# Attention scratch and SiLU results moved from PSUM to SBUF in a two-layer token kernel

## What is computed

```python
kx = modulated_linear(x, s, k_aff_w, k_aff_b, k_w, k_b).reshape(B, N, H, D)
scores = einsum('bnhd,bnjd->bnhj', kx, kx) / sqrt(D)       # 16 x 16 for each token
A = softmax(scores, axis=-1)
out = einsum('bnhj,bnjd->bnhd', A, kx).reshape(B, N, F)
x = x + modulated_linear(out, s, o_aff_w, o_aff_b, o_w, o_b)
...
x = x + _ln(silu(cat @ int_W1 + int_b1) @ int_W2 + int_b2) # cat: the six parts
```

## Time and profile before

| | us |
|---|---|
| median of three runs | 875.09 |
| lowest and highest of the three | 874.53, 875.51 |
| the profiled execution, measured from outside | 875.09 |
| its span, from the first to the last instruction | 873.2 |

### The profile page before, as it was taken

One profiled execution on the slowest core, in us unless ns is written; L12 is line 12 of the kernel. 1 busy time (PEld: TensorE's weight loads), 2 busy tenths in 40 slices (PEclk: granted clock), 3 DMA queues, 4 the chain that ended last, 5 costly groups with the idle time before them and its releaser, 6 DMA issues.

```text
span 873.2 us, 19685 instructions
## 1 busy us (share of the span) xinstructions
PE 843.7 (97%) x7456; PEld 768.8 (88%) x7474; DVE 644.7 (74%) x1067; ACT 488.3 (56%) x851; POOL 608.1 (70%) x766
## 2 busy tenths in 40 slices
PE   5996999999999999999999999999999999999997
PEld 5854888989999998989999898999999898999986
DVE  3589777778787867679797877679797767677652
ACT  3567555565656465465656556465647546464531
POOL 2377999678786766768776866768777775756472
PEclk9898999999999999999999999999999999999999
DMA  8972234425343333425243332424333342323110
GB/s 285 418 255 61 71 86 119 115 57 153 77 153 84 98 92 85 127 50 158 69 149 89 108 92 73 115 71 146 83 122 91 86 116 49 104 67 82 47 50 25
DMA packets 104365, 95.55 MB, mean 109 GB/s; under 512 B 72880, under 2 KB 78160, under 8 KB 102608
## 3 DMA queue, kind: packets, MB, share of 16 engines
q1 hardware_dynamic: 95056, 69.26, 27.6%
q0 software_dynamic: 4608, 16.78, 7.0%
q10 hardware_dynamic: 4608, 8.25, 2.8%
HBM read 69.60 MB, written 8.40 MB: 89 GB/s over the span
## 4 chain that ended last, share of the span: by engine, by line
PE 91%; DVE 4%; DMA 2%; issue 1%; ACT 1%; ACTq 0%; SPq 0%; POOL 0%; another core or an unknown queue 0%; DVEq 0%; POOLq 0%
PE acc L399 45%; PE tok L399 29%; PE att L399 8%; PE xp L552 6%; PE xp L399 3%; DMA kb<-in_kb 1%; DVE stg_e L1277 1%; DMA BD<-q 0%; DVE raw_k L1164 0%; SPq L297 0%; DVE W1xl L1267 0%; DVE q L1290 0%; DVE BD L1179 0%; DVE qt L1283 0%
## 5 line engine op out<-in xcount | busy, mean ns | idle before, releaser
L1699 POOL TENSOR_TENSOR op1l<-ytmp,op1h 128x512 fp32r<-128x512 f32 x64 | 90.3, 1411 | 20.8 <-ACT op1h L906 20.4
L1645 POOL TENSOR_TENSOR xlo<-xraw,xhi 128x512 fp32r<-128x512 f32 x31 | 40.8, 1317 | 68.6 <-ACT xhi L798 68.6
L399 PE MATMUL acc<-op0h,W1xh 128*128 128x256 f32 x256 | 75.8, 296 | 1.4 <-DVE op0l L1369 1.1
L399 PE MATMUL acc<-op1h,W1th 128*128 128x256 f32 x256 | 75.0, 293 | 0.0
L399 PE MATMUL acc<-op1h,W1hh 128*128 128x256 f32 x256 | 73.7, 288 | 0.0
L399 PE MATMUL acc<-op0h,W1sh 128*128 128x256 f32 x256 | 73.7, 288 | 0.0
L399 PE MATMUL acc<-op1h,W1tl 128*128 128x256 f32 x256 | 72.4, 283 | 0.0
L399 PE MATMUL acc<-op1l,W1hh 128*128 128x256 f32 x256 | 72.4, 283 | 0.0
L399 PE MATMUL acc<-op1l,W1th 128*128 128x256 f32 x256 | 72.4, 283 | 0.0
L399 PE MATMUL acc<-op0h,W1sl 128*128 128x256 f32 x256 | 72.4, 283 | 0.0
L399 PE MATMUL acc<-op0l,W1sh 128*128 128x256 f32 x256 | 72.4, 283 | 0.0
(11 more groups left out here) (269 smaller groups left out, 3048.9 us busy)
## 6 DMA issues: line engine op xcount, KB each, us to landing
xsq<-in_x SPq DMA_DIRECT2D x32, 256.0 KB, 3.1
xb<-in_x SPq DMA_DIRECT2D x32, 256.0 KB, 3.0
out<-xb SPq DMA_DIRECT2D x32, 256.0 KB, 2.4
BD<-q SPq DMA_DIRECT2D x124, 64.0 KB, 2.1
BD<-v SPq DMA_DIRECT2D x124, 64.0 KB
xraw<-in_xT SPq DMA_DIRECT2D x30, 256.0 KB, 3.0
ring<-in_k_wT ACTq DMA_DIRECT2D x6, 256.0 KB, 3.5
dmb<-dm_rows SPq DMA_DIRECT2D x6, 256.0 KB, 3.9
```

The source lines that it names most:

```text
L399: return e.matmul(o, a, b, start=start, stop=True, skip_group_check=True)
L1645: e.tensor_tensor(xlo[:, :, :], (xraw1 if g == 1 else xraw)[:, :, :], xhi[:, :, :].bitcast(F32), ALU.subtract).then_inc(s["xlo"], 1)
L1699: e.tensor_tensor(op[slot]["l"][:, :, half(g)], four(ytmp[YT[n, g][0]]), op[slot]["h"][:, :, half(g)].bitcast(F32), ALU.subtract).then_inc ...
```

## The change

The attention scratch leaves PSUM. score_low and value_low become one helper, sum_part, which copies half by half, each half when its semaphore comes, with no mask. score_sum adds the mask instead: two instructions on DVE with att as one input and SE as the other, written to SE. The row maximum, the subtraction, the exponential, the row sum and the normalisation all work in place in SE; the transpose goes to the SBUF tile ET, and e_first and e_second read ET. SiLU writes a ytmp tile instead of acc, and its rounding and silu_lo read that tile. The list of ytmp uses gets two entries more for each pair, so that the slots of all the others stay the same. PE waits for SiLU alone (sil), not for silu_lo (asl), before it writes acc again. Subtractions that were TENSOR_TENSOR become SCALAR_TENSOR_TENSOR with a factor of 1.0.

```diff
@@ y_uses
-        yield from [("h", pa), ("h", pb), ("t", a), ("w", pa), ("w", pb)]
+        yield from [("h", pa), ("h", pb), ("sil", pa), ("sil", pb), ("t", a), ("w", pa), ("w", pb)]
@@ W1_part, and the same in id_rows
-                        e.wait_ge(s["asl"], 2 * (k - 1) + pair + 1)
+                        e.wait_ge(s["sil"], 2 * (k - 1) + pair + 1)
@@ ACT
-            def score_low(g):
-                e.wait_ge(s["S"], 2 * g + 2)
...
-                for t in range(2):
-                    e.activation(by_token(SE)[:, :, t, :], scored(1)[:, :, t, :], ACT.Identity, bias=cst[:, 16 + t:17 + t]).then_inc(s["Sc"], 1)
+            def sum_part(g, of, to):
+                for h in range(2):
+                    e.wait_ge(s[of], 2 * g + h + 1)
...
+                    e.copy(SE[:, h * 256:h * 256 + 256], att_half(h, 1)).then_inc(s[to], 1)
...
-                e.activation(att[:, 0:512], SE[:, :], ACT.Exp, scale=SCALE).then_inc(s["exp"], 1)
+                e.activation(SE[:, :], SE[:, :], ACT.Exp, scale=SCALE).then_inc(s["exp"], 1)
...
-                e.copy(e12[:, :, 0], att[:, 512:1024]).then_inc(s["e1"], 1)
+                e.copy(e12[:, :, 0], ET[:, :]).then_inc(s["e1"], 1)
@@ silu
-                y = ps[f"acc{pair}"]
+                y = take_y(e, ("sil", n))
                 e.wait_ge(s["W1h"], n + 1)
-                e.activation(y[:, :], y[:, :], ACT.Silu).then_inc(s["sil"], 1)
+                e.activation(y[:, :], ps[f"acc{pair}"][:, :], ACT.Silu).then_inc(s["sil"], 1)
@@ DVE: score_sum
-                e.tensor_tensor(high, high, SE[:, :], ALU.add).then_inc(s["Ss"], 1)
+                for t in range(2):
...
+                    e.scalar_tensor_tensor(out=c, in0=a, scalar=cst[:, 16 + t:17 + t], in1=c, op0=ALU.add, op1=ALU.add).then_inc(s["Ss"], 1)
@@ less_max
-                e.tensor_tensor(by_head(SE[:, :]), by_head(high), mx.unsqueeze(2).to_broadcast([128, 16, 32]), ALU.subtract).then_inc(s["sub"], 1)
+                e.scalar_tensor_tensor(out=by_head(SE), in0=by_head(SE), scalar=1.0, in1=mx.unsqueeze(2).to_broadcast([128, 16, 32]), op0=ALU.mult, op1=ALU.subtract).then_inc(s["sub"], 1)
@@ e_T
-                e.scalar_tensor_tensor(out=by_head(SE[:, :]), in0=by_head(att[:, 0:512]), scalar=UP, in1=rden.unsqueeze(2).to_broadcast([128, 16, 32]), op0=ALU.mult, op1=ALU.mult).then_inc(s["ET"], 1)
+                e.scalar_tensor_tensor(out=by_head(SE), in0=by_head(SE), scalar=UP, in1=rden.unsqueeze(2).to_broadcast([128, 16, 32]), op0=ALU.mult, op1=ALU.mult).then_inc(s["ET"], 1)
                 e.wait_ge(s["ET"], 2 * g + 1)
-                e.transpose(att[:, 512:1024], SE[:, :]).then_inc(s["ET"], 1)
+                e.transpose(ET[:, :], SE[:, :]).then_inc(s["ET"], 1)
@@ e_second
-                e.tensor_tensor(e12[:, :, 1], att[:, 512:1024], e12[:, :, 0], ALU.subtract).then_inc(s["e2"], 1)
+                e.scalar_tensor_tensor(out=e12[:, :, 1], in0=ET[:, :], scalar=1.0, in1=e12[:, :, 0], op0=ALU.mult, op1=ALU.subtract).then_inc(s["e2"], 1)
```

More of the change, by code:

```diff
@@ L64, in y_uses @@
         yield from [("t", pb), ("s", pa), ("s", pb)]
-        yield from [("h", pa), ("h", pb), ("t", a), ("w", pa), ("w", pb)]
+        yield from [("h", pa), ("h", pb), ("sil", pa), ("sil", pb), ("t", a), ("w", pa), ("w", pb)]
     pa, pb = NG - 2, NG - 1
-    yield from [("t", pb), ("s", pa), ("s", pb), ("h", pa), ("h", pb), ("w", pa), ("w", pb)]
+    yield from [("t", pb), ("s", pa), ("s", pb), ("h", pa), ("h", pb), ("sil", pa), ("sil", pb), ("w", pa), ("w", pb)]
 XP = rotate(xp_uses(), 2)
@@ L1304, in w_T @@
                 e.transpose(wT[g % 2][:, :], w32[g % 2][:, :]).then_inc(s["wt"], 1)
[L1306 removed]
             def score_sum(g):
                 e.wait_ge(s["Sc"], 2 * g + 2)
[L1311 removed]
+                for t in range(2):
+                    c = SE[:, :].rearrange("p (k t m) -> p k t m", t=2, m=16)[:, :, t, :]
+                    a = att[:, :].rearrange("p (k t m u) -> p k t m u", t=2, m=16, u=2)[:, :, t, :, 0]
+                    e.scalar_tensor_tensor(out=c, in0=a, scalar=cst[:, 16 + t:17 + t], in1=c, op0=ALU.add, op1=ALU.add).then_inc(s["Ss"], 1)
             def less_max(g):
[L1314 to L1315 removed]
+                e.wait_ge(s["Ss"], 2 * g + 2)
+                e.tensor_reduce(mx, by_head(SE), axis=AX.X, op=ALU.max).then_inc(s["sub"], 1)
                 e.wait_ge(s["sub"], 2 * g + 1)
[L1317 removed]
+                e.scalar_tensor_tensor(out=by_head(SE), in0=by_head(SE), scalar=1.0, in1=mx.unsqueeze(2).to_broadcast([128, 16, 32]), op0=ALU.mult, op1=ALU.subtract).then_inc(s["sub"], 1)
             def e_T(g):
                 e.wait_ge(s["exp"], g + 1)
[L1322 removed]
+                e.tensor_reduce(den, by_head(SE), axis=AX.X, op=ALU.add).then_inc(s["rd"], 1)
                 e.wait_ge(s["rd"], 2 * g + 1)
@@ L1388, in silu_lo @@
                 e.wait_ge(s["ash"], n + 1)
-                e.tensor_tensor(op[0]["l"][:, c, :].rearrange("p a b -> p (a b)"), ps[f"acc{pair}"][:, :],
-                                op[0]["h"][:, c, :].rearrange("p a b -> p (a b)").bitcast(F32), ALU.subtract).then_inc(s["asl"], 1)
+                e.scalar_tensor_tensor(out=op[0]["l"][:, c, :].rearrange("p a b -> p (a b)"), in0=ytmp[YT["sil", n][0]][:, :], scalar=1.0,
+                                       in1=op[0]["h"][:, c, :].rearrange("p a b -> p (a b)").bitcast(F32), op0=ALU.mult, op1=ALU.subtract).then_inc(s["asl"], 1)
             def last_stats(g):
```

44 lines of the change are left out of this document (18 added, 26 removed).

## The result

| | before | after |
|---|---|---|
| median, us | 874.81 (4 runs) | 886.71 (4 runs) |
| lowest to highest | 873.41 to 875.51 | 886.13 to 887.53 |
| span of the profiled execution | 873.2 | 887.9 |

The kernel after is slower: ratio 1.0140, 95% interval 1.0118 to 1.0161. By the medians that is 11.9 us, by the ratio 12.2. The direction and the range (875 to 887) held, the range by 0.3 us only; the forecast of 879.4 us had 4.3 us where 11.9 were measured. The profiled execution of after is some 3 us longer than the median (887.9 + 1.9 around it), so its terms add up to 14.7 us and not to 11.9.

What follows compares the result with a forecast made beforehand. PE was taken to bound the loop, busy 727.8 of 730.0 us. Stalls of 0.8 + 0.8 + 2.1 + 0.6 = 4.3 us on 875.09 us gave 879.4 us, range 875.0 to 887.0.

Steps and rivals of the forecast that it cites:

- Part 1: Operation lengths: path from scores to e_second 0.1 to 0.5 us shorter, hidden in the loop; both splits unchanged.
- Part 2: Four kinds of DVE operation, 32 each, get two SBUF inputs; each starting behind POOL is late by up to 1.2 us.
- Part 3: ACT's SiLU table load starts 1.0 us later, and SiLU with it; in a plain iteration 1.77 us before W2_part covers it.
- Part 4: Places where slack is too small for the delays: stalls of 0.8 + 0.8 + 2.1 + 0.6 = 4.3 us.
- Iteration 1: Groups 2 and 3: e_second caught late by POOL operations, so PE stalls at values, 0.8 us each.
- the subtraction is caught too: High case for group 2 of the first iteration: stall 1.3 us, against 0.2 to 0.3 from normalisation and e_second alone.
- The iterations with mod_scale: In 3, 7 and 11, late silu_lo falls behind x_lo and W2_part's second half waits 0.7 us each, 2.1 in all.
- the lost race: Rival: second silu_lo falls behind x_lo in the 11 other iterations too, 7.7 us more, 887 us; chance 0.17.
- POOL is pushed everywhere: Rival: POOL's low parts 0.5 us late in each of 14 iterations, 886 us; counted with the rival above, together 0.17.
- Iteration 15: u_make, behind SiLU and a softmax caught by POOL's affine, comes late; u_T stalls 0.6 us, between 0 and 0.7.
- Not slower: Rival: slack absorbs all the delays, sum 0 to 1.7 us, 875 to 876.8 us; chance 0.21.
- PE's busy time in the loop: Sign to look for in the profile after: PE's busy time in the loop stays at 728 us.

Runs made afterwards that it cites:

- e6: Kernel before with copies by halves, mask in score_sum and the new instruction form, but results and one input kept in PSUM, SiLU too: 874.83 us, ratio 0.9996.
- e2: Kernel before with the SiLU part alone (SiLU to ytmp, late table load), attention scratch still in PSUM: 876.01 us, ratio 1.0007.
- e4: Kernel before with one more wait ahead of SiLU, so the table load starts 1.0 us later: 875.34 us, ratio 0.9996.
- e3: Kernel after with SiLU's wait for its ytmp slot moved ahead to e_first, so the table load waits for nothing: 885.95 us, ratio 1.0112.
- e9: Kernel after with the attention scratch of groups 0 to 3 (preamble and iteration 1) in PSUM as before: 884.85 us, ratio 1.0105.
- e1: Kernel after with its SiLU part undone (SiLU in place in acc), attention scratch still in SBUF: 880.85 us, ratio 1.0063.
- e10: Kernel after with POOL's mod_scale cut from 512 columns to one, all instructions and signals kept: 881.76 us, ratio 1.0074.
- e5: Kernel after with one more wait: POOL's x_lo behind the second silu_lo waits for that silu_lo: 884.32 us, ratio 1.0101.
- e12: e1 with e4's wait added, so the table load is late while silu_lo still reads acc in PSUM: 881.12 us, ratio 1.0071.

## Why the prediction was right or wrong

**Part 1, lengths: right.** Copies take 371 ns. The two halves of score_sum take 0.47 us each, overlap, and need 0.84 together (at 120.85 in the kernel after), 0.16 more than the old sum. The other forms on DVE keep their length within 0.02 us, and e6 shows that copies, mask and form are worth nothing. That both splits stay the same was not right for their half on ACT, which takes 0.03 us longer (last section). By the Trainium skill, page "VectorE: DVE Perf Modes", section "The TRN2 errata — SBUF-src ops pay a fixed extra latency per instruction", each operation should save an estimated 65 ns. The traces show 5: the maximum takes 686 ns from SBUF (after) and 691 from PSUM (e6). The measurement decides.

**Part 2, the wait for POOL: right in kind.** Of the 128 operations with two new SBUF inputs 63 took over 0.9 us in the trace after, and every one of them ended 0.54 to 0.64 us behind the end of a POOL operation. POOL's next one, if it had 512 columns, took 1.62 to 1.76 us where it followed at once. Seven more took 0.69 to 0.79 us because they started late in a POOL operation, and ended 0.55 to 0.58 us behind it. By the Trainium skill, page "SBUF — State Buffer", section "SBUF: two separate sides", a whole instruction of one excludes the other's. The traces agree but for two things: an operation that takes 0.69 us alone ends 0.54 us behind POOL's, so some 0.1 us of the two overlap; and one did not wait at all, a subtraction at 46.22 that ran its 0.69 us inside a POOL operation on 12 columns (44.74 to 47.00). Over all the traces in which the four kinds have two SBUF inputs, 488 of them start inside a POOL operation of 512 columns, and 487 of these end at least 0.54 us behind its end; in the one left (e2, 631.25, 0.05 us behind x_lo's start) it was POOL that waited, 1.86 us. What I had not allowed for: 4 of the 63 missed the first boundary and waited for a second POOL operation too, the longest of them for 2.80 us.

**Part 3, the load: right, and incomplete.** The timeline of after in iteration 9 answers to the earlier trace rows.

```profile
535.08 0.28 PE L392 MATMUL acc<-op1h,W1hl 128*128 128x256 f32 x1
...
535.45 1.28 ACT L908 ACT_TABLE_LOAD   x1 [0.38 <-PE acc L392]
```

The load starts 0.09 us behind the end of the half's last matmul, 1.1 us later against PE than before. Alone it costs nothing (e4). The slack that I gave it (1.77 us in iteration 7) was real, but the load, the softmax ahead of it and the catch all draw on it. And in iterations 3, 7 and 11, where I used it, the load is not what makes silu_lo late: there it starts right behind e_first, which the softmax has delayed, and with the load early (e3) W2_part is as late as without.

**Part 4, where slack is too small: this step failed, in three ways.**

- *Iteration 1, 0.8 + 0.8 against 4.5 in the profile and 3.1 by e9.* Of the 4.5, 1.4 us are the lower clock, which the kernel before has ahead of the loop (last section). In e1, e3 and e10, whose traces have it there too, iteration 1 is 2.2 to 2.4 us longer than before: PE is 0.6 to 0.7 us late at values of group 2 and 1.7 to 2.0 more at those of group 3, of which some 1.0 comes back where the kernel before waits 1.38 us itself (129.84, transpose of u). So the term that was too small is group 3's, and the clock's place is missing from the sum. For group 2 I took the middle between "two catches" and "the subtraction is caught too". In the kernel after it is caught: 1.37 us at 93.23, inside POOL's split of 92.74, and so are the normalisation (1.34) and e_second (1.39). An operation that starts inside one of POOL's is not perhaps late. In group 3 the subtraction takes 2.80 and not 0.69, the normalisation 1.47, e_second 1.38; I had one catch of 1.0 in the sum.
- *The iterations with mod_scale, 2.1 against 5.1 in the profile and 5.7 by e10.* I named the mechanism of iteration 7 (catch by mod_scale, then the lost race), but priced only the second half's 0.7, and put the first silu_lo's lateness on the load where it is the softmax's (part 3). Measured are both halves: 0.46 and 0.44. And I looked for it only in 3, 7 and 11. POOL has mod_scale at the end of iterations 2, 6 and 10 as well, 1.7 us earlier against PE; once the attention has pushed POOL back by 1.1 us, these meet silu_lo too. In before they don't, so a search for overlaps in the trace of before couldn't find them: the list had to be shifted first.
- *"POOL is pushed everywhere" was put among the rivals, as 0.5 us in each of 14 iterations.* It is true, and it costs little by itself (e1: iterations 5, 6, 9, 10, 13 and 14 are within 0.02 us of before). It acts through the place of mod_scale.

**Iteration 15: right in size, in part by luck.** The timeline of after answers to the earlier trace rows: u_make ends at 838.68 and the transpose starts at once, 0.7 to 0.8 us late (0.6 predicted). I put it on one catch of the softmax. But in e1's trace, which has the attention's catches without the SiLU part, the transpose isn't late, and in e2's, with the SiLU part alone, it is 0.4 us late. In e9's trace it is 0.4. No run takes the two apart in the kernel after.

```profile
837.87 0.81 ACT L867 ACTIVATE pgb<-pgb,nm,small 128x512 f32<-128x512 f32 x1
...
838.73 0.66 PE L545 MATMUL xp<-ident,pgb 128*128 128x128 f32 x4 [0.55 <-ACT pgb L867]
```

**Not foreseen:** 0.5 in iteration 2, 0.6 in 12 and 1.3 us on the projection of x in 4, 7, 8 and 12. They are single handovers of 0.3 to 0.6 us behind a delayed POOL, ACT or DVE, in the profiled execution; no experiment took them apart. What the preamble costs can't be told from single profiles: the loop starts between 90.6 and 94.5 us in the traces of the kernels here.

**The rivals.** The lost race came true in 3, 7 and 11, where I had it, and in three of the eleven others (2, 6 and 10), each time behind mod_scale: in a plain iteration the second silu_lo keeps its 0.25 us (after, iterations 5 and 9), since it waits for DVE's own transpose, as the prediction said against it. "Not slower" fails by the intervals. Of the signs that I named, PE's busy time in the loop did not stay at 728 us: it is 734.6, since missing overlaps and the clock go into it.

## What to carry to other kernels

A DVE operation with both inputs in SBUF waited for the POOL operation of 512 columns that ran, in 487 of 488 cases here, so count for each such operation the start, the POOL operation it falls into, and the end 0.55 us behind it; a busy POOL makes this the common case (63 of 128 here at 71% busy). Give one input a place in PSUM, or keep the operations out of chains with less slack than all their catches added. Delays of one chain and of the lists that they push use the same slack: shift the lists first, then look for overlaps, and expect that two edits can cost more together (12.2) than apart (5.5 and 0.6). A late start in one profile can belong to the clock: see where the other kernel has its low stretch before you give it to the change.

## What the runs showed of the hardware that was not expected

**The clock after a wait.** In iteration 1 of the kernel after, PE waits 1.93 us for e_second ahead of values. The timeline, and the windows from there (PE's granted clock is the third number from the end):

```profile
101.91 1.65 PE L392 MATMUL att<-e,BD 128*128 128x64 f16 x32 [1.93 <-DVE e L1323]
```

```profile
99.00:101.00 2.00, 0.98 (x11) 0.76 (x9) 1.74 (x3) 1.24 (x2) 2.00 (x2) 1.00 0.89 244
101.00:103.00 2.00, 1.09 (x26) 1.12 (x27) 0.76 (x1) 0.26 (x1) 2.00 (x3) 0.83 0.05 19
103.00:105.00 2.00, 2.00 (x18) 2.00 (x16) 1.40 (x3) 1.52 (x5) 1.92 (x2) 0.50 0.03 8
105.00:107.00 2.00, 2.00 (x16) 2.00 (x16) 1.97 (x5) 1.04 (x2) 1.72 (x2) 0.82 0.00 0
```

The clock goes from 2.4 to 1.2 GHz (1.00 to 0.50) after the wait and is back within about 4 us. In that time a matmul of 0.28 us takes 0.41, and PE's list falls back 1.4 us more, beside the wait itself. I had put no such term into iteration 1. In e1, where the wait at the same place is 0.40 us, the clock stays at 1.00.

It is not simply a price of the change. The kernel before has such a stretch just ahead of the loop, behind a wait of 2.75 us; the kernel after waits 1.82 us there and has none. The timeline of before, its window from 88 us, and that of after:

```profile
88.56 1.09 PE L552 MATMUL xp<-ident,xb 128*128 128x128 f32 x4 [2.75 <-DVE op0l L1369]
```

```profile
88.00:92.00 4.00, 3.44 (x12) 2.96 (x13) 3.87 (x7) 2.31 (x5) 3.72 (x5) 0.57 0.12 15
```

```profile
88.00:92.00 4.00, 2.18 (x13) 1.56 (x12) 3.97 (x8) 1.00 (x3) 3.67 (x6) 1.00 0.00 0
```

Laid beside the kernel before, the kernel after is 1.8 us late at 88 us and 0.5 at 92.5: it wins there about what the clock takes from it in iteration 1, and its early PE also has the longer wait for e_second. The mean granted clock is 0.986 in both traces. By the start of iteration 2, PE is 3.5, 3.8 and 4.4 us late in e1, e3 and e10, which have the stretch at 90 to 94 us and waits of 0.40 to 0.49 us for e_second of group 2, and 5.0, 4.3 and 3.4 us late in after, e5 and e12, which have it at 101 to 106 us, behind waits of 1.90 to 1.93 us. So the place of the stretch moves a loss from one row of the table of terms to another, and says nothing sure about the total. Part of the spread between executions of the kernel after may be whether this happens; that was not measured.

**ACT's operations get a little longer in SBUF.** The groups by form of after: e_first, which now reads SBUF, and the exp, which read SBUF before too and now writes it.

```profile
L840 ACT CAST e<-ET 128x512 f16<-128x512 f32 x32 | 25.1, 783 | 41.4 <-DVE ET L1319 41.4
...
L834 ACT ACTIVATE SE<-SE 128x512 f32<-128x512 f32 x32 | 20.3, 633 | 55.1 <-POOL SE L1654 55.1
```

The same two in the kernel before, with PSUM in the place of SBUF:

```profile
L850 ACT CAST e<-att 128x512 f16<-128x512 f32 x32 | 24.1, 752 | 24.1 <-DVE att L1328 24.1
...
L844 ACT ACTIVATE att<-SE 128x512 f32<-128x512 f32 x32 | 19.3, 602 | 43.9 <-POOL SE L1663 43.9
```

That is 31 ns each; the rounding of SiLU's result goes from 587 to 623 ns. No run here prices these by themselves.
